# A tile's gates on ScalarE, dummy products around the first transposes, two weight units rounded earlier

## The reference

```python
x = x + tanh(g_xattn) * retention(layernorm(x), ctx, ctx, Wq, Wk, Wv)   # masked, decaying scores, no softmax
xf = layernorm(x)
scores = softmax(xf @ Wg.T)
expert_weights, expert_indices = top_k(scores, 2)
expert_weights = expert_weights / expert_weights.sum(-1)
h1 = xf @ W1[e].T + low_rank(A1[e], B1[e]) + b1[e]
h3 = xf @ W3[e].T + low_rank(A3[e], B3[e]) + b3[e]
g  = silu(h1) * h3
y_e = g @ W2[e].T + low_rank(A2[e], B2[e]) + b2[e]
x = x + tanh(g_ffn) * sum(gate[e] * y_e for the two chosen experts e)
```

## Time and profile before

| What | Value |
|---|---|
| Median of 3 runs | 340.1 us (339.66 to 343.45) |
| Profiled execution | 340.37 us, span of its instructions 338.5 us |
| Mean granted clock of TensorE | 0.969 of full speed |
| TensorE busy | 301.8 us, 89% of the span |
| VectorE busy | 262.0 us, 77% |
| ScalarE busy | 190.5 us, 56% |
| GpSimd busy | 209.9 us, 62% |

### The profile page before, as it was taken

The page is one execution under the profiler, slowest core; times in us unless marked ns, Lnnn a source line. Parts: engine busy times, 40 slices in busy tenths (PEclk is TensorE's granted clock), DMA queues, the critical chain, the costliest instruction groups (busy, mean ns, idle before and its releaser), DMA issues.

```text
span 338.5 us, 7418 instructions
## 1 busy us (share of the span) xinstructions
PE 301.8 (89%) x1738; PEld 231.8 (68%) x1758; DVE 262.0 (77%) x685; ACT 190.5 (56%) x406; POOL 209.9 (62%) x245
## 2 busy tenths in 40 slices
PE   8589979799997878987999989999999999999970
PEld 4468858698885644765677757777777777777750
DVE  2679886798999979897799897777778767877750
ACT  4646664576878437565565364455555644664540
POOL 1459795788892094877375656565666765766341
PEclk9899997999999699999999999999999999999995
DMA  7947798898974274565575766776652233234100
GB/s 243 397 129 220 212 261 249 254 293 266 301 226 160 57 227 141 186 191 136 129 198 167 182 189 172 185 200 192 154 127 35 46 60 63 38 54 63 17 0 0
DMA packets 30423, 54.34 MB, mean 161 GB/s; under 512 B 7232, under 2 KB 15808, under 8 KB 30112
## 3 DMA queue, kind: packets, MB, share of 16 engines
q1 hardware_dynamic: 16128, 38.99, 35.3%
q0 software_dynamic: 7488, 9.36, 16.7%
q10 hardware_dynamic: 6768, 5.54, 5.2%
HBM read 41.92 MB, written 10.65 MB: 155 GB/s over the span
## 4 chain that ended last, share of the span: by engine, by line
PE 44%; DVE 16%; DMA 12%; POOL 8%; issue 8%; ACT 4%; SPq 3%; DVEq 2%; POOLq 1%; ACTq 0%
PE bank L614 21%; PE bank L631 11%; DMA stage<-w_all_in 5%; POOL WL L911 5%; PE bank L622 3%; DMA out<-ys,cols 3%; DMA WH<-lora_in 2%; DVE stage L1020 2%; PE bank L604 2%; DMA LS<-WH 2%; DVE g L1423 1%; SPq L349 1%; DVE h L1423 1%; DVEq L1403 1%; PE bank L548 1%
## 5 line engine op out<-in xcount | busy, mean ns | idle before, releaser
L990 POOL DMA_INDIRECT out<-ys,cols x39 | 63.5, 1628 | 64.0 <-PE bank L604 23.0
L911 POOL TENSOR_TENSOR WL<-stage,WH 128x512 bf16<-128x512 f32 x48 | 61.6, 1327 | 18.0 <-ACT WH L723 17.5
L614 PE MATMUL bank<-WH,xh 128*128 x156 | 55.7, 438 | 0.7 <-ACT xh L837 0.6
L975 POOL DMA_INDIRECT xg<-xn_rows,colg x39 | 41.6, 1066 | 21.1 <-DVE colg L1251 10.8
L614 PE MATMUL bank<-WH,xl 128*128 x156 | 49.0, 395 | 0.0
L614 PE MATMUL bank<-WL,xb 128*128 x137 | 42.9, 384 | 1.3
L723 ACT ACTIVATE WH<-stage 128x512 fp32r<-128x512 f32 x48 | 29.5, 630 | 21.5 <-DVE stage L1020 20.3
L874 ACT ACTIVATE ys<-BA,gsel 128x256 f32 x23 | 11.7, 509 | 43.4 <-DMA out<-ys,cols 43.4
L1020 DVE TENSOR_TENSOR stage<-bank,stage 128x512 f32<-128x512 f32 x48 | 31.4, 680 | 5.8 <-DMA stage<-w_all_in 5.2
L631 PE MATMUL bank<-WH,gh 128*128 x156 | 31.8, 325 | 2.9 <-ACT gh L843 2.9
L614 PEld LDWEIGHTS bank<-WH,xl 128*128 128x128 f32 x156 | 29.2, 188 | 7.2 <-DVE xl L1413 0.4
(11 more groups left out here) (221 smaller groups left out, 659.5 us busy)
## 6 DMA issues: line engine op xcount, KB each, us to landing
stage<-w_all_in SPq DMA_DIRECT2D x48, 256.0 KB, 4.0
BB<-biases_in SPq DMA_DIRECT2D x16, 640.0 KB
BA<-biases_in SPq DMA_DIRECT2D x8, 640.0 KB
LS<-WH SPq DMA_DIRECT2D x45, 48.0 KB
cx<-ctxT_in SPq DMA_DIRECT2D x8, 256.0 KB, 4.9
out<-x ACTq DMA_DIRECT2D x8, 256.0 KB, 3.6
xn_rows<-xn ACTq DMA_DIRECT2D x8, 256.0 KB, 5.4
xs<-x_in SPq DMA_DIRECT2D x6, 256.0 KB, 3.7
```

The costliest lines, as they stand in the source:

```text
L614: last = nc.tensor.matmul(dst[:, :], lhs[p][:, c * P:(c + 1) * P], W[:, bass.ds(e * (UNITS * UC) + (2 * kind + c) * UC, HID)], start=(part ...
L911: nc.gpsimd.tensor_tensor(w_dst(WL, s, m), stage[(u * UNITS + m) % NSTAGE][:], w_dst(WH, s, m).bitcast(F32), ALU.subtract).then_inc(s_wl, 1)
L975: nc.gpsimd.indirect_dma_start(out=xg[q][:], out_offset=None, in_=xn2_d[0:JA * P, :] if i < NA else xn2_d, in_offset=bass.IndirectOffsetOn ...
L990: nc.gpsimd.indirect_dma_start(out=out_rows, out_offset=bass.IndirectOffsetOnAxis(ap=cols[:, i:i + 1], axis=0), in_=ys[p][:], in_offset=No ...
```

## The change

The gates are computed by ScalarE, each as one activation: the first is a copy of the table's column scaled by the row's gate number, the second an identity with scale and with the first gate as its bias. ScalarE reads the tile's number at the beginning of each tile, does the first gate behind the two copies of x and the second behind Silu, and for the tile itself instead of the next one. The twelve dummy products become five ahead of the first transposes, into another bank and without the wait for x2, and four behind them. Units 0 and 1 of the last expert are rounded ahead of Silu of tile 0 instead of behind the stores. An activation of one element a row with Silu stands ahead of the loop.

```diff
@@ tensor
             unit(E - 1, 1, 1)
-            pe.wait_ge(s_x2, B)
-            keep_clock(12, WL, pO)
+            keep_clock(5, WL, pS)
...
             x_transposes(0, 0)
+            keep_clock(4, WL, pS)
             pe.wait_ge(s_wl, (E - 2) * UNITS + 4)
@@ scalar
+            def first_gate(i, q, v):
+
+                act.wait_ge(s_xg[q], 16 * ((i - q) // XBUF + 1))
+                pos_wait(act, s_gs, i)
+                is0 = is0A if i < NA else is0B
+                nc.scalar.activation(g0, is0[:, bass.ds(v, 1)], ACT.Copy, scale=xg[q][:, D:D + 1]).then_inc(s_g0, 1)
+
+            def both_gates(i, q, v):
+
+                is1 = is1A if i < NA else is1B
+                act.wait_ge(s_g0, i + 1)
+                pos_wait(act, s_ys, i - XBUF + 1)
+                nc.scalar.activation(gs[q], is1[:, bass.ds(v, 1)], ACT.Identity, scale=xg[q][:, D + 1:D + 2], bias=g0
+                                     ).then_inc(s_gs, 1)
+
             def tile(i, q, first, more):
                 p = q % 2
+                if i == 0:
+                    act.wait_ge(s_routed, 1)
+                if i == NA:
+                    act.wait_ge(s_routed, 2)
+                v = act.value_load(vid[0:1, i:i + 1], min_val=0, max_val=NV - 1)
                 if not first:
                     g_high(i - 1)
                 if more:
                     x_parts(i + 1, 1 - p)
+                first_gate(i, q, v)
                 if not first:
                     g_short(i - 1)
...
+                if i == 0:
+                    weight_hi(E - 1, 1, 0)
+                    weight_hi(E - 1, 1, 1)
                 act.wait_ge(s_h1b, i + 1)
                 nc.scalar.activation(h1[:], h1[:], ACT.Silu).then_inc(s_silu, 1)
+                both_gates(i, q, v)
...
                     store_rows(B - 1)
-                    weight_hi(E - 1, 1, 0)
-                    weight_hi(E - 1, 1, 1)
...
             deviation(B - 1)
+            nc.scalar.activation(junk2, eps_t[:], ACT.Silu)
             tile_steps(act, tile)
@@ vector
-            def gates_of(i, q):
...
-                if more:
-                    gates_of(i + 1, (q + 1) % XBUF)
                 beside_h1(i)
...
             variance(st2, mv2, s_mv2, sums(x2, st2))
-            dve.wait_ge(s_routed, 1)
-            gates_of(0, 0)
             x_rest(0, 0)
```

More of the change, by code:

```diff
@@ L308, in flamingo @@
         kj1 = spare(KJ, BF16)
-        junk = spare(1, F32)
+        junk, junk2 = spare(1, F32), spare(1, F32)
         kjA = spare(KA * NV, BF16).rearrange("p (w v) -> p w v", v=NV)
```

## The result

The changed kernel takes **339.44 us** (median of 20 runs, 334.93 to 342.2) beside 340.43 us of the kernel before on the same chip (20 runs); the ratio is 0.9917, with an interval of 0.9889 to 0.9945. Measured again it was 340.11 us (12 runs) beside 341.42 (29 runs), 0.9972 [0.9936, 1.0008]. A ratio counts only executions within 1.5% of the fastest of their kernel, in the first measurement eleven of the changed kernel's twenty but eighteen of the twenty before, so 0.9917 flatters the change. The gain is small: 1.0 and 1.3 us by the medians, 2.8 by the first ratio; the interval of the first ratio is clear of 1, that of the second is not. 4.5 us were forecast.

What follows compares the result with a forecast made beforehand. TensorE's own work was taken to bound 200 to 322 us, leaving 8.5 us of gaps from 118 to 200 to win. Terms 2.1 + 1.2 + 0.55 + 0.8 - 0.55 - 0.2 + 0.6 = 4.5 gave 335.9 us, range 333.8 to 339.3.

Steps and rivals of the forecast that it cites:

- tile 2 (start, capped by BB): First tiles: gh 2.65 us sooner, but tile 2's bias load follows the second store, so 2.1 us remain won.
- gaps of 150.07 and 153.36: TensorE waits for a product a GpSimd pair delayed; with that pair earlier they just miss: 1.2 plus 0.55 us won.
- gap of 159.38: TensorE waits for gh behind a scatter and GpSimd's third pair; that pair sooner, 0.8 of 1.24 us won.
- gap of 170.63: ScalarE's read of the tile number stands behind a DMA issue before gh: 0.55 us lost, bounds 0 and 0.7.
- gap of 198.02: gl stood behind VectorE's last routing step; without gates and their read that starts sooner: 0.6 us won.
- full tiles: The read fits ScalarE's 0.74 us idle before gh; gates shift gb and Silu: 0.2 us lost in all.
- the step on the third pair: GpSimd's third rounding pair for the last expert, at 146.37, comes 2.1 to 4.5 us sooner; 3.9 taken.
- rival A: GpSimd's pairs hit other VectorE products and the gain is given back: 1.5 us won, 338.9 us; chance 0.18.
- rival B: ScalarE becomes the bound between ys and gh, 0.3 us late in each of 25 full tiles: 343.4 us; chance 0.06.
- C: With fewer dummies TensorE's clock drops to 1.2 GHz for 5 us at the start: 341 us; chance 0.05.
- D: Tile 0's bias load or the gathers, not VectorE, hold its h; only later terms come: 338.0 us; chance 0.14.

Runs made afterwards that it cites:

- The read early: Changed kernel with the number of the next tile read behind the second gate, ahead of the wait for ys: 339.62 us, 0.9915 of the kernel before.
- all but the gates: Changed kernel with the gates still on VectorE, all other edits kept: 341.78 us, 0.9997 of the kernel before.
- two reads: Changed kernel with ScalarE's read of the tile number done twice in a row in every tile: 345.17 us, 1.0120 of the kernel before.
- gates alone: Kernel before with the gates moved to ScalarE and nothing else of the change: 343.62 us, 1.0054 of the kernel before.

## Why the prediction was right in its start and too high in its sum

The gain was forecast at 4.5 us; it is 1 to 2.8. The forecast of 335.9 us was 3.5 too low, and the median lies just above the range; the ratio of 0.9917 on 340.1 us would be 337.3, inside, but that ratio flatters the change. The first term held; most of the later ones did not. The terms, measured as differences in the table, each from single executions (changed; changed again):

| Term | predicted | measured |
|---|---|---|
| tile 2 (start, capped by BB) | +2.1 | +1.99; +2.07 |
| gaps of 150.07 and 153.36 (tile 2 to 3) | +1.75 | +0.55; +0.43 |
| gap of 159.38 (tile 3 to 4) | +0.8 | -0.58; -0.43 |
| gap of 170.63 (tile 4 to 6) | -0.55 | -0.78; -0.79 |
| tile 6 to 8 | 0 | -0.14; -0.17 |
| gap of 198.02 (tile 8 to 12: 82.44 before, 80.10 and 81.02) | +0.6 | +1.30; +0.31 |
| full tiles (12 to 38) | -0.2 | -1.38; -1.20 |
| sum | 4.5 | 0.96; 0.22 |

- **Start: right.** First products 3.37 us after the mark (3.16 expected), h of tile 0 5.12 (4.9), Silu 7.05 (7.1), second store 9.97 (9.7), tile 2 capped by its bias load. At tile 0 I expected 2.65 and got 1.94: the second store came 1.76 us sooner instead of 2.05, and behind the DMA issues the read left 1.90 us of idling where 1.04 stood before, 0.86 instead of 0.55. Tile 2 met its 2.1 partly by luck: the store explains 1.76 us of it, the rest came with a bias load that landed sooner (7.08 us from the second store to h of tile 2 instead of 7.63, a stretch that varies from trace to trace).
- **Within it, one credit was wrong.** I counted the two units moved away from gh as 1.15 us won. Put back, they make tile 0 1.15 us sooner: they had run beside the read there, and ahead of Silu they delay all that follows.
- **Gap of 150.07: the step on the third pair failed.** "I take 3.9, for the first scatters had been behind the pairs": the first pair did move, but the second and third stand behind scatters and the third came 26.53 - 23.99 = 2.5 us sooner, near the lower bound of 2.1. The product still met the pair and took 2.34 us instead of 2.82. This is rival A's collision, and of the 1.75 us credited it left 0.55 and 0.43; the start, which A would have eaten too, stayed.
- **Gap of 159.38: wrong in sign.** "Of 1.24 I keep 0.8": I let gh follow the scatter, with the third pair about four us sooner. The pair came 2.5 us sooner and ys of tile 4 2.49, while TensorE was ready 2.77 us sooner: the scatter gave this gap nothing, and the read added 0.50 us between ys and gh, where a table load and the Exp stood before too. The read early takes 0.6 us off the gap (2.05 to 1.45), and with the Exp moved too it vanishes.
- **Gap of 170.63: right in sign, mis-sized,** 0.8 instead of 0.55; it lay just outside my bound of 0.7.
- **Full tiles: open.** The table shows 1.2 to 1.4 us lost, yet the kernel without dummies, whose ScalarE does the same, loses none. Single executions differ by this much in when scatters land, and the 119.97 us of the one trace before is at the low end. That the read costs these tiles is not shown: all but the gates, with no read on ScalarE, took 121.89 us from tile 13 on. With two reads they took 124.23, more than any other trace: rival B was one read away.
- **C and D did not come.** The clock is 1.00 from 118 to 133 us. It had risen by 117.5 us, before the first dummy (118.33); that the dummies keep it up is likely, but only the one execution without them speaks for it. Not VectorE's gates alone held the start: in the times nothing is gained without the other edits, and without the gates neither.
- **Prices.** The two gates took 0.305 and 0.388 us, means of 39 each. From the Trainium skill, page "ScalarE: Activation LUTs", section "What ACT_TABLE_LOAD costs", come the estimates of 0.28 and 0.37; the trace nearly agrees. VectorE's products with two inputs in SBUF took 2.71, 2.59 and 2.34 us beside GpSimd's pairs. The Trainium skill, page "SBUF — State Buffer", section "Who interferes with whom", has the one that starts second wait wholly for the other. The rows of 2.59 and 2.34 agree: the product starts after the pair has begun and ends 0.56 us after the pair. In the row of 2.71 the product starts 0.17 us ahead of the pair by the profile and waits all the same, which the rule does not give.

## What to carry to other kernels

Ahead of the instruction that the busiest engine waits for, count everything on the releasing engine that does not need the late input, reads of registers and table loads too, and move it ahead of the wait: by the medians that was worth 2.4 to 3.6 us here, the change itself 1.0 to 1.3. Before crediting a moved step, ask what it had been hiding (here a read) and what it now stands in front of (here Silu). When several waits hang on one event, freeing one shows only the next.

## What was not expected of the hardware

A read of a number into a register cost ScalarE 0.53 us behind another read, 0.21 behind an activation of 0.51 us, and nothing that shows behind 1.15 us of activations; behind two DMA issues it added 0.86. A low clock lasts: after the small routing products TensorE stayed at 1.2 GHz until about 127 us without dummies, until 117 to 122 us in most other traces, and in the one with the gates alone until 125, though its twelve dummies ran. It also falls again within the tiles, and not in every execution: behind waits for gh of 2.47 us (two reads) and 2.00 us (gates alone) in tile 4 it was at 1.2 GHz for more than 3 us, behind those of 2.05 and 1.91 us of the changed kernel it stayed at 2.4.
